# Causal attention in half-steps: the order of the products ST, PV and S on TensorE, and a wait of ScalarE

## What is computed

```
q = einsum('bthc,oc->btho', xh, Wq) * scale     # scale = 256 ** -0.25, same for k
k = einsum('bthc,oc->btho', xh, Wk) * scale
v = einsum('bthc,oc->btho', xh, Wv)
scores = einsum('bihc,bjhc->bhij', q, k)
scores = where(j > i, -inf, scores)
attn = softmax(scores, axis=-1)
y = einsum('bhij,bjhc->bihc', attn, v)
return y @ Wu.T + bu
```

## Time and profile before

| | us |
|---|---|
| median of 3 runs | 2200.34 |
| lowest, highest | 2199.07, 2216.99 |
| span of the profiled execution | 2206.0 |
| of it, attention (about 110 to 1560) | 1450 |

### The profile page before, as it was taken

One profiled execution on the slowest core, in us unless ns is written; L12 is line 12 of the kernel. 1 busy time (PEld: TensorE's weight loads), 2 busy tenths in 40 slices (PEclk: granted clock), 3 DMA queues, 4 the chain that ended last, 5 costly groups with the idle time before them and its releaser, 6 DMA issues. The chain is left out here.

```text
span 2206.0 us, 44494 instructions
## 1 busy us (share of the span) xinstructions
PE 2061.7 (93%) x17787; PEld 1095.9 (50%) x17787; DVE 1693.4 (77%) x2102; ACT 1433.2 (65%) x2797; POOL 578.3 (26%) x827
## 2 busy tenths in 40 slices
PE   7899999999999999999999999999988597999996
PEld 5343333334444444344444433333337486888886
DVE  7688886999999878899999988876628674555553
ACT  5256765778888877678888888888755132344432
POOL 2021110110111111111110100000025563777777
PEclk9699987999999999999999999999979598999999
DMA  6442310111611111441121111000019253555552
GB/s 235 116 83 51 66 37 20 57 57 43 105 58 46 60 41 44 84 75 46 58 70 36 53 49 32 11 1 2 2 55 343 103 183 122 120 117 124 119 124 53
DMA packets 127634, 170.88 MB, mean 77 GB/s; under 512 B 17745, under 2 KB 97106, under 8 KB 126658
## 3 DMA queue, kind: packets, MB, share of 16 engines
q1 hardware_dynamic: 111424, 146.07, 23.8%
q0 software_dynamic: 14016, 17.45, 4.4%
q10 hardware_dynamic: 1986, 4.51, 0.5%
HBM read 91.53 MB, written 77.60 MB: 77 GB/s over the span
## 5 line engine op out<-in xcount | busy, mean ns | idle before, releaser
L848 DVE TENSOR_REDUCE mx<-S 128x2 f32<-128x1024 f32 (+3 forms) x1152 | 1281.7, 1134 | 224.3 <-PE S L744 146.6
L824 ACT ACTIVATE prob<-ST 128x512 f32<-128x512 f32 (+3 forms) x2304 | 1168.6, 559 | 335.8 <-PE ST L765 289.9
L791 PE MATMUL O<-prob,V 128*17 128x256 f32 (+1 forms) x8704 | 678.9, 385 | 0.2 <-POOL prob L713 0.2
L744 PE MATMUL S<-K,Q 48*128 48x512 f32 (+3 forms) x2304 | 562.0, 485 | 25.4 <-DVE mx L848 19.1
L765 PE MATMUL ST<-Q,K 49*128 49x512 f32 (+3 forms) x2304 | 488.4, 420 | 37.3 <-ACT prob L824 31.7
L744 PEld LDWEIGHTS S<-K,Q 48*128 48x128 f32 x2304 | 219.2, 187 | 457.7 <-issue 290.5
L713 POOL TENSOR_SCALAR_AFFINE_SELECT prob<-prob 128x512 f32<-128x512 f32 x128 | 81.2, 635 | 1048.1 <-ACT prob L824 1048.1
L765 PEld LDWEIGHTS ST<-Q,K 49*128 49x128 f32 x2304 | 220.3, 187 | 146.0 <-ACT prob L824 105.1
L791 PEld LDWEIGHTS O<-prob,V 128*17 128x17 f32 x8704 | 145.0, 95 | 281.4 <-issue 272.0
L1622 ACT ACTIVATE sg<-hg 128x512 f32<-128x512 f32 x92 | 55.0, 598 | 160.4 <-PE hu L1550 160.4
L1478 POOL DMA_INDIRECT out<-yo,idt x76 | 122.3, 1609 | 21.4 <-issue 19.0
(11 more groups left out here) (231 smaller groups left out, 1867.8 us busy)
## 6 DMA issues: line engine op xcount, KB each, us to landing
cwb<-cwt SPq DMA_DIRECT2D x76, 256.0 KB, 3.9
lists<-wbd SPq DMA_DIRECT2D x132, 138.0 KB, 2.3
Q<-qs SPq DMA_DIRECT2D x192, 64.0 KB, 2.4
xs<-lists SPq DMA_DIRECT2D x19, 552.0 KB, 3.8
K<-ks SPq DMA_DIRECT2D x18, 512.0 KB, 9.3
wraw<-in_wcat SPq DMA_DIRECT2D x54, 128.0 KB, 2.1
whi_parts<-wcut SPq DMA_DIRECT2D x54, 128.0 KB, 2.1
wlo_parts<-wcut SPq DMA_DIRECT2D x54, 128.0 KB, 2.0
```

The costliest lines, as they stand in the source:

```text
L744: ins = pe.matmul(out[:, ab, 0:w], Q[g, n % QR, p, r * P:(r + 1) * P], K[G % 2][g, p, c * BW:c * BW + w], start=True, stop=not diag)
L791: ins = pe.matmul(O[32 * a:32 * a + VC, c0:c1], V[:, G, k, VC * a:VC * (a + 1)], prob[:, s % NP, a, c0:c1], start=s in FIRST and h == 0, s ...
L824: act.activation(prob[:, s % NP, 2 * p + ab, c0:BW], ST[i % ST_BANKS][:, c0:BW], ACT.Exp).then_inc(s_exp, 1)
L848: dve.tensor_reduce(mx[:, n % 2, a:a + step + 1:step, c], S[slot % S_RING][:, :, 0:w], AX_X, ALU.max).then_inc(s_free, 1)
```

## The change

In each half-step of `attention_order` the S jobs (`scores`) are now put ahead of the PV pieces (`weigh`), in both halves. `closing`, called in the arguments of `scores`, moves along. In ScalarE's part the wait for `s_pv` goes. Nothing else is changed: the same instructions with the same shapes.

```
@@ attention_order
         events.append(("ST", (s, 0)))
+        scores(s + 0.5, closing(s + 0.5))
         weigh(s, PIECES_BEFORE[s - 1] if s >= 2 else 0)
-        scores(s + 0.5, closing(s + 0.5))
         events.append(("ST", (s, 1)))
         if s in LAST:
             ask(LAST.index(s) + 1)
+        scores(s + 1, closing(s + 1))
         weigh(s, PIECES_BEFORE[s - 1] + 1 if s >= 1 else 0)
-        scores(s + 1, closing(s + 1))
@@ attend, ScalarE
                         c0 = query_start(j, k)
-                        if s >= NP:
-                            need("pv", s_pv, PIECES_BEFORE[s - NP + 1])
                         for ab in range(2):
```

## The result

The changed kernel is slower: 2231.31 us (median of 4, 2220.11 to 2238.41) against 2204.32 for the kernel before (4 runs), ratio 1.013 with a 95% interval of 1.0084 to 1.0175. The forecast was 2188.

A forecast was written before the change was run, and what follows sets the result against it. Attention was read as paced by TensorE's half-step of about 1.22 us, VectorE and ScalarE close, plus late ST loads through ScalarE's loop. −10 − 3 − 5 + 6 + 3 − 3 = −12 us: 2188 on the median, range 2168 to 2206.

The forecast's parts named there:

- The steady step: Regular attention half-steps: ScalarE's loop falls to 1.18 us, below TensorE's 1.22, and the late ST load goes; −10 us.
- my first two terms: Regular half-steps lose the late ST load, −10 us; TensorE's other waits of ST for ScalarE shrink, −3 us.
- Block ends: Last two PV of a block now stand side by side: 1.87 to 1.66 us, 25 places, −5 us.
- Narrow ST: Half-steps with ST of 128 to 384 columns: ST no longer covers S's load; +6 us, upper bound +19.
- Short PV: Two half-steps per block with a 128-column PV: nothing in front hides ST's load; +3 us (0 to +5).
- Diagonal: Masked diagonal scores: short S now lies behind wide ST, 0.01 us for each of 256 jobs; −3 us.
- MT and YO: Row of maxima and turned output: move by 0.2 us with two steps to spare; no cost put down.
- The clock: Half-clock stretches: an uncertainty of all cases; one more or fewer moves the time by some 17 us.
- Rival 3: ST's waits lose their cover behind PV, ScalarE's loop exceeds 1.22 us: about +30, 2230 us; chance 0.07.
- under 60 us: Sign that the forecast is right: idle time before ST's load falls from 105 us to under 60.
- rival 4: ST's load is pulled ahead under PV, 0.19 us less in some 1,000 half-steps: −90, 2110 us; chance 0.02.
- Rival 1: VectorE takes over, its reductions pacing half-steps at 1.22 us: no change, 2200 us; chance 0.18.

The follow-up runs named there:

- e1: Kernel before with only ScalarE's second wait removed, its order kept: ratio 0.9937 to the kernel before, 2203.3 us at 200 us of half clock.
- e5: The changed kernel run again, 10 executions on chip B: ratio 1.0069 to the kernel before, 2196.3 us at 200 us of half clock.
- e13: The changed kernel run once more, 12 executions on chip B: ratio 1.0079 to the kernel before, 2195.3 us at 200 us of half clock.
- e4: Changed kernel with the old order (PV first) in half-steps with MT or YO: ratio 0.9932 to the kernel before, 2190.6 us at 200 us of half clock.
- e8: As e4, but early filler products kept to the end of the fourth block instead of the second: 2209.5 us at 200 us of half clock, no ratio.
- e16: Changed kernel with PV ahead of MT and the first two blocks in the old order: median 2181.2 us, ratio 0.9874 to the kernel before.
- e6: Changed kernel with the old order in half-steps with MT or YO and in the first two blocks: ratio 0.9946 to the kernel before.
- e10: Changed kernel with PV ahead of YO only, chip C: ratio 1.0128 to the kernel before, 2200.9 us at 200 us of half clock.
- e9: Changed kernel with PV ahead of MT only, 4 executions on chip C: 2185.9 us at 200 us of half clock, no ratio.
- e15: Changed kernel with PV ahead of MT only, 7 executions on chip B: ratio 0.9886 to the kernel before, 2186.2 us at 200 us of half clock.
- e7: Kernel before with MT or YO and S put ahead of PV in those half-steps alone, old wait kept: ratio 1.0468 to the kernel before.

## Why the prediction was wrong

*The steady step: right, its size good.* ScalarE's loop became 0.54 + 0.60 + 0.05, and the half-steps of the regular kind went from 1.251 to 1.224 us on the mean (561 and 569 of them at full clock): −15 us for the −13 of my first two terms. e1 shows that the second wait did stand between ST's semaphore and the exponential.

*Block ends, right:* 1.90 to 1.66 us, 25 times: −6 for −5. The Trainium skill (TensorEngine Tiling (Array Packing), "Key Properties") says that a change of the way the array is split drains it; by that rule a PV pair should cost less than two PVs apart, and the trace agrees: 0.99 against twice 0.56.

*Narrow ST, wrong sign:* +6 was put down. The half-steps stayed at 1.15 us for 128 columns and fell for 256 (1.18 to 1.12) and 384 (1.19 to 1.17): −0, −0.06 and −0.02 at 64 each, −5 us. The second load lies 0.11, not 0.20 us behind the first. *Short PV:* 1.11 to 1.19 us, +5 for +3. *Diagonal:* for a score of 512, 384, 256 and 128 keys 1.363 to 1.352, 1.289 to 1.278, 1.251 to 1.259 and 1.192 to 1.186 us, so about −0.01 for 256 jobs, −2 for −3.

*MT and YO, a term left out.* "The row of maxima and the turned output move by 0.2 us, with two steps to spare": I asked only whether they come in time, and put their own half-steps at nothing. The half-step with MT grew from 1.89 to 2.00 us and that with YO from 1.83 to 1.95, about +7 us in all. It isn't mainly a longer wait: at the turn shown above (2.01 to 2.05) the wait behind MT fell by 0.13 us, while the product behind ST (MT now, PV before) follows after 0.43 instead of 0.35 us, and the product behind S (PV now, ST before) after 0.42 instead of 0.34. With it the sum is −15 − 6 − 5 + 5 − 2 + 7 = −16; measured at equal half clock −16.0 (e5) and −17.0 (e13). Forecast −12. So all but the clock came out near the forecast, partly by errors that cancel (narrow ST 11 us too high, MT and YO 7 too low).

*The clock, the step that failed.* "One more or one fewer such stretch moves the time by that": I priced it well (17 us for 44 us; 44 × 0.37 = 16) but took it for chance that belongs to all cases alike. It hangs on the change: 302 and 317 us at half clock against 193 on chip B, 116 × 0.37 = +43 us by the means. That turned −16 into a loss. Rival 3 named 2230, next to the 2231.31 measured, but that is luck; it went another way: it wanted ST to wait behind PV. It doesn't; TensorE's own waits for ScalarE are 30.2 us after 31.7:

```profile
PE ST L765 <- ACT prob L822: 30.2, 65, 0.8
```

The load path shows instead

```profile
PEld ST L765 <- ACT prob L822: 480.6, 1046, 1.1
```

where I had asked for under 60 us. That was a misreading of the view: most of these 1,046 are the idle 0.42 us that belongs to any load behind PV, which the earlier trace rows put under "issue" for S and which now bears the name of what came last. PV to ST stayed at 0.56, so rival 4 fell too: the Trainium skill's pull-ahead (TensorE: Matmul & The Clock Gate, "The mechanism") doesn't show for a load behind PV; there the trace disagrees in both orders. Rival 1 fell with 1.224 against 1.251.

*What stays open.* Why the clock is lower in the new order, where TensorE waits no more than before, wasn't found. The low stretch at the start is long in the new order although TensorE is busy 81.27 of its 81.90 us, so idle time isn't what keeps it there. Most other low stretches of both kernels begin some 30 us behind a turn (318.2 before, 932.5 after); that place wasn't tested apart. Nor does a run tell what the regular half-steps of the new order do by themselves: e4 has them at 210 us of half clock, as before (211), but with 6.2 us of those waits instead of 19.1. What more products early on do stays open too (e8). And YO is better left ahead of PV at equal half clock (e16 lies 6.9 us below e6; e10 is 8.9 us below before, the changed kernel 16 to 17), though its own half-step is shorter behind PV (1.85 against 2.09); what the regular half-steps lose by it (1.231 against 1.224) wasn't traced further.

## What to carry to other kernels

When a product is put behind another on an in-order engine, price the rare half-steps too, and look at what stands between two users of a shared slot: e4, e9 and e15 have one more PV there and take 6 to 10 us less than the changed kernel at equal half clock. In a kernel like this one, whose clock falls several times in a run, don't take the time at half clock for chance: read the clock of each execution and compare kernels at equal time at half clock; the gain of 16 us would otherwise have stayed unseen under the loss. And before a wait is blamed for a lower clock, add it up in the kernel before as well. And a second semaphore on an instruction isn't free where the first one arrives last: 479 of them cost 10 us here.

## What the runs showed of the hardware that I had not expected

- A waiting instruction with two semaphores on ScalarE: the separate semaphore instruction waited for the later signal (ST's), and the exponential started only behind it (for the exponential that starts at 1002.48 in the earlier trace rows, the semaphore instruction starts at 1002.42). Start of the exponential after ST's load: 0.62 before, 0.54 after, in the first half of a step.
- The order of the same products moved the time at 1.2 GHz by over 100 us (193 to 302 and 317 on the mean), without more waiting of TensorE for VectorE. Within the new order, filling the waits of up to 0.9 us at the turns took 61 us of it away (317 to 256), and in e7, where the waits of S add up to 30.6 us, it was 408. The Trainium skill (TensorE: Matmul & The Clock Gate, "A second HAM failure mode: psum-queue depth-cycling") describes a kernel whose TensorE idles briefly between groups of products, often enough that the clock swings between its two levels. The trace of e7 agrees; the kernel before, with 19.1 us of such waits and little half clock, shows that the sum of the waits alone doesn't decide it.
- The same kernel ran with 131 to 287 us at half clock on one chip, and its time (2187 to 2247 us) follows from that on a straight line, with a scatter of 2.3 us (standard deviation) around it.
